# Delta-rule chunk outputs: adding the masked product onto the query's product in PSUM, with the sum copied by ScalarE

## Chip, cores and metric

One core of one Trainium2 chip. The metric is the device time of one execution in microseconds (us); given are the median of three runs of the kernel before and one profiled execution.

## What is computed

A hybrid block on x of 8 x 1024 x 128 floats: delta-rule attention, a mixture of 8 experts (top 2), a linear recurrence, and the experts again, each on a layer-normed x and added to it. The change touches the delta rule alone. Per batch row and head (4 heads, keys of 16, values of 32) the reference goes through the sequence in chunks with a state S:

```
def step(S, xs):
    qc, kc, vc, bc = xs
    kb = kc * bc[:, None]
    A = jnp.tril(kb @ kc.T, -1)
    U = solve_triangular(eye + A, vc * bc[:, None] - kb @ S, lower=True)
    o = qc @ S + jnp.tril(qc @ kc.T) @ U
    return (S + kc.T @ U, o)
```

Then o is normalised per head, multiplied by a gate, projected and added to x. The kernel cuts the sequence into chunks of 32, which gives the same outputs.

## The kernel before

Eight groups of 128 positions of all eight batch rows go through a software pipeline. An iteration i of it has 42 slots (SLOTS), and for each slot every engine runs, in a fixed order written out in its own loop, the pieces of several groups that are due in that slot: the state's chunks of group i (`stage_c`), the routing of group i-1 to the experts (`stage_r`, from iteration 1 on), what follows the state (`post`), the triangular inverse of group i+1 (`row_of_inverse` and `stage_b` on VectorE, `apply`), projections and grams of group i+2 (`stage_a`) and layer norm and convolution of group i+3 (`stage_l`). The tables from L_VAR to R_SEND (lines 339 to 382) say in which slot a piece stands. No scheduler moves anything: each engine works strictly through its own list, and semaphores do the rest.

A group has four chunks, which start in slots 2, 11, 24 and 29 (C_AT), in the last group in 2, 6, 10 and 14. One chunk goes like this:

- slot +0 (k = 0), TensorE L1675: 32 small matmuls of 32 x 32 weights give w S (columns WS0, 0 to 63) and q S (columns QS0, 64 to 127) in PSUM banks 0 to 3. It waits for the state (`d_S`) and for the copy of the chunk before (`d_oq`).
- slot +0, VectorE L868: vp = u - w S.
- slot +0, ScalarE L1354: when vp is done, copy q S from PSUM to `oq` (`d_oq`).
- slot +2, TensorE L1686 (KV): the state's product k^T vp into columns 0 to 63 of the same banks, after `d_vp` and `d_oq`; not for the last chunk of all. Then L1698 (PV): the masked product gp vp into bank 4 (BK_O), which it shares with the transposes of wk (L1658).
- slot +2, VectorE L874: S = masked KV + S, two instructions (`d_S`).
- slot +6 (in the last group +3), VectorE L880: o = oq + PV.

Later ScalarE squares o (L1369), VectorE reduces it, multiplies it with the gate (L895) and with the inverse norm (L899), TensorE turns and projects it (L1712, L1717), VectorE adds it to x (L905).

Beside this stand the pieces that the prediction follows. VectorE computes the inverse of group i+1 row by row: in slots 1 to 15 a product (L817) and a reduction (L821), with the state's pieces written between the two; in eight later slots the block products (L826 to L844). ScalarE in slot 14 writes the eight routing rows of group i-1 (L1271, `ysc`), in slot 16 rounds a piece of the experts' weights (L1405, `hl`; VectorE's L1063 follows), in slot 17 copies the turned rows (L1383, `yTf`); TensorE's router (L1739) follows, and VectorE takes its logits in slot 18 (L915, `lg`). In slot 27 ScalarE copies the turned queries of group i+2 (L1327, `qT`) and makes the masked `kqm` (L1329); TensorE's convolution (L1594) of group i+3 in slot 30 needs these to be out of PSUM bank 7, and it stands ahead of the fourth chunk's slot +2. In slots 34, 35, 36 and 40 TensorE makes the grams (L1630), which VectorE reads (L798, L800).

Of the kernel before, what the change touches and what calls it, by code (L numbers as in the profile page):

```python
# [80 lines left out]
def hybrid_kernel(nc, ap, out, phases=4):  # L81
# [37 lines left out]
    with ctx:  # L119
# [108 lines left out]
        S = sb1("S", [2, Q, 2 * DV])  # L228
        oq = sb1("oq", [2, 2, HEADS * DV])
        u = sb1("u", [2, BPB, HEADS * DV])  # L230
# [131 lines left out]
        C_S = 2  # L362
        C_PV = 2
        C_O = (6, 3)
        P_SQ = ((30, 1), (10, 18))
# [361 lines left out]
        def _(ve):  # L727
# [128 lines left out]
            def stage_c(g, t):  # L856
                for c in range(CG):
                    k = t - C_AT[last(g)][c]
                    at = g * CG + c
                    both = slice(2 * c, 2 * c + 2)  # L860

                    def by_pair(v):
                        return v.rearrange("p n (a d) -> p (n a) d", d=2 * DV)

                    if k == C_V:
                        ve.wait_ge(s("d_ws"), at + 1)
                        ve.wait_ge(s("d_uw"), at + 1)
                        ve.tensor_tensor(by_pair(vp[:, at % 2]), by_pair(u[:, g % 2, both]), ps[:, 0:4, WS0:WS0 + 2 * DV],  # L868
                                         ALU.subtract).then_inc(s("d_vp"), 1)
                    if k == C_S and at + 1 < NCK:  # L870
                        ve.wait_ge(s("d_kv"), at + 1)
                        for h in range(2):
                            cols = slice(DV * h, DV * h + DV)
                            ins = ve.scalar_tensor_tensor(S[:, (at + 1) % 2, :, cols], ps[:, 0:4, KV0 + DV * h:KV0 + DV * h + DV],  # L874
                                                          head_of[:, h, 0:1], S[:, at % 2, :, cols], ALU.mult, ALU.add)
                        ins.then_inc(s("d_S"), 1)
                    if k == C_O[last(g)]:
                        ve.wait_ge(s("d_pv"), at + 1)
                        ve.wait_ge(s("d_oq"), at + 1)
                        ve.tensor_tensor(o[:, g % 2, both], oq[:, at % 2],  # L880
                                         ps[:, BK_O, 0:2 * P].rearrange("p (n d) -> p n d", n=2), ALU.add)\
                            .then_inc(s("d_o"), 1)

            def post(g, half, t):
# [3 lines left out]
                if t == P_SS[last(g)][half]:  # L888
# [4 lines left out]
                        .then_inc(s("d_oss"), 1)  # L893
                if t == P_GATE[last(g)][half]:
                    marks["gs"] = ch.mark(ve.tensor_tensor(gs4, gs4, o4, ALU.mult))  # L895
                if t == P_O[last(g)][half]:
# [358 lines left out]
        def _(act):  # L1255
# [91 lines left out]
            def stage_c(g, t):  # L1347
                for c in range(CG):
                    if t == C_AT[last(g)][c] + C_V:
                        at = g * CG + c  # L1350
                        act.wait_ge(s("d_vp"), at + 1)
                        if at >= 2:
                            act.wait_ge(s("d_o"), at - 1)
                        act.copy(oq[:, at % 2].rearrange("p n (a d) -> p (n a) d", d=2 * DV), ps[:, 0:4, QS0:QS0 + 2 * DV])\  # L1354
                            .then_inc(s("d_oq"), 1)

# [216 lines left out]
        def _(pe):  # L1573
# [24 lines left out]
            def stage_a(g, t):  # L1598
# [23 lines left out]
                if t in A_GRAM:  # L1622
# [3 lines left out]
                    if g >= 2 and c == 0:  # L1626
                        pe.wait_ge(s("d_S"), (g - 1) * CG + 1)
                    for j in range(Q):
                        for a in range(4):
# [5 lines left out]
            def apply(g, late, t):  # L1635

                for k in range(2):
# [16 lines left out]
                    if t == WT[order][k]:  # L1654
                        pe.wait_ge(s("d_uw"), at + 1)
                        pe.wait_ge(s("d_wTs"), at)
                        pe.wait_ge(s("d_o"), g * CG + max(c - 1 - last(g), 0))
                        pe.transpose(ps[:, BK_O, 0:P], wk[:, c % 2].rearrange("p n d -> p (n d)"), ident[:, :])\  # L1658
# [6 lines left out]
            def chunk(g, c, k):  # L1665
                at = g * CG + c
                if k == 0:
                    pe.wait_ge(s("d_S"), at + 1)
                    pe.wait_ge(s("d_wTs"), at + 1)
                    pe.wait_ge(s("d_oq"), at)  # L1670
                    pe.wait_ge(s("d_gp"), min(g + 2, B) * CG)
# [6 lines left out]
                if k == C_KV:  # L1678
                    pe.wait_ge(s("d_vp"), at + 1)
                    pe.wait_ge(s("d_oq"), at + 1)  # L1680
                    if at + 1 < NCK:
# [7 lines left out]
                        ins.then_inc(s("d_kv"), 1)  # L1689
                if k == C_PV:  # L1690
                    pe.wait_ge(s("d_vp"), at + 1)
                    pe.wait_ge(s("d_o"), at)
                    pe.wait_ge(s("d_wTs"), g * CG + min(c + 2 + last(g), CG))
                    for n in range(2):
                        for h in range(HEADS):
                            k0 = n * P + h * DV
                            for j in range(Q):
                                ins = pe.matmul(ps[rows_of(j), BK_O, k0:k0 + DV], gp[rows_of(j), g % 3, 2 * c + n, h, :],  # L1698
                                                vp[rows_of(j), at % 2, n, h * DV:h * DV + DV], start=True, stop=True,
                                                skip_group_check=True)  # L1700
                    ins.then_inc(s("d_pv"), 1)

# [245 lines left out]
```

## Time and profile before

| | |
|---|---|
| median of 3 runs | 1392.16 us (1390.52 to 1394.14) |
| the profiled execution | 1395.43 us, its span 1393.5 us |
| mean granted TensorE clock | 0.802 of full |
| busy share of the span | TensorE 72%, VectorE 79%, ScalarE 51%, GpSimd 57% |
| last start of a chunk's vp | 556.2 us into the span |

The delta stage fills about the first 575 us. How to read the rows below: a timeline row has start, duration, engine, line, operation, output<-inputs, shape and count; in brackets the idle time of that engine just before it and who ended it. PE is TensorE, PEld its weight loads, DVE VectorE, ACT ScalarE, POOL GpSimd; L numbers are lines of the kernel before. TensorE's ends are modelled. Several like instructions in a row are merged into one row.

### The profile page before, as it was taken

To read this page: it belongs to the slowest core of one execution; us is meant where nothing else is said; L and a number is where in the kernel's file an instruction comes from. 1 tells how busy PE (TensorE), PEld (TensorE's weight loads), DVE (VectorE), ACT (ScalarE), POOL (GpSimd) and SP (SyncE) were. 2 spreads that over 40 slices of the span, in tenths; PEclk is the share of its full clock that TensorE was granted. 3 is DMA by queue.
4 is the path that set the end of the run, shared out by engine and by line. 5 is a ranking of instruction groups with operands and counts; after the bars stand their busy time and mean duration, and the time that the engine had idled before them with its cause. 6 is when DMAs were issued, how large, how long until landed. Compare 5 with 4: busy or idle time off the path is not lost.

```text
span 1393.5 us, 33043 instructions
## 1 busy us (share of the span) xinstructions
PE 997.9 (72%) x11963; PEld 732.8 (53%) x11963; DVE 1099.6 (79%) x3207; ACT 717.0 (51%) x1534; POOL 789.7 (57%) x670
## 2 busy tenths in 40 slices
PE   4547778677686546799999955656554699999960
PEld 1214455545555444678888842323232478788850
DVE  1188899989999894589788845898988689888845
ACT  2434253443534211467677735656565367677740
POOL 3331346556665544467777651158777747777650
PEclk9778778595876555699999986776676699999985
DMA  5010111111211104059778832122111659788839
GB/s 137 23 46 25 35 38 60 36 49 40 67 53 36 58 15 179 26 199 306 254 274 296 280 114 90 33 83 73 34 37 40 217 189 291 249 286 282 284 107 349
DMA packets 78625, 184.34 MB, mean 132 GB/s; under 512 B 16735, under 2 KB 44826, under 8 KB 68224
## 3 DMA queue, kind: packets, MB, share of 16 engines
q1 hardware_dynamic: 51280, 142.04, 30.5%
q0 software_dynamic: 17280, 35.70, 7.3%
q10 hardware_dynamic: 9904, 4.49, 1.2%
q8 instruction: 97, 1.59, 0.5%
q14 instruction: 64, 0.52, 0.1%
HBM read 131.20 MB, written 52.79 MB: 132 GB/s over the span
## 4 chain that ended last, share of the span: by engine, by line
PE 31%; DVE 28%; POOL 15%; issue 12%; ACT 7%; DMA 4%; SPq 1%; POOLq 0%; DVEq 0%; ACTq 0%
POOL xs L647 6%; PE ps L1594 5%; POOL res L690 5%; POOL rn L630 2%; PE ps L1810 2%; PE ps L1812 2%; PE ps L1811 2%; PE ps L1822 2%; PE ps L1824 2%; PE ps L1823 2%; DVE prod L817 2%; DVE t_p L821 2%; ACT ysc L1271 1%; DVE r_stats L739 1%; DVE hidl L1129 1%
## 5 line engine op out<-in xcount | busy, mean ns | idle before, releaser
L690 POOL DMA_INDIRECT res<-orow,idt x284 | 294.1, 1036 | 126.1 <-issue 80.6
L647 POOL DMA_INDIRECT xs<-ysc,slot_u x256 | 283.2, 1106 | 144.7 <-issue 72.8
L1129 DVE TENSOR_TENSOR hidl<-hidf,hidh 128x512 fp32r<-128x512 f32 (+1 forms) x320 | 199.1, 637 | 22.7 <-ACT hidh L1456 16.9
L1454 ACT ACTIVATE hidf<-ps,wb 128x512 f32<-128x512 f32 (+1 forms) x320 | 198.3, 655 | 5.0 <-PE ps L1812 4.4
L1810 PE MATMUL ps<-yTh,wb 128*128 128x512 f32 (+1 forms) x320 | 126.8, 396 | 0.0
L1822 PE MATMUL ps<-hidh,wb 128*128 128x512 f32 (+1 forms) x320 | 124.6, 389 | 0.0
L1812 PE MATMUL ps<-yTh,wb 128*128 128x512 f32 (+1 forms) x320 | 119.3, 373 | 0.0
L1811 PE MATMUL ps<-yTl,wb 128*128 128x512 f32 (+1 forms) x320 | 119.0, 372 | 0.0
L1824 PE MATMUL ps<-hidh,wb 128*128 128x512 f32 (+1 forms) x320 | 117.8, 368 | 0.0
L1823 PE MATMUL ps<-hidl,wb 128*128 128x512 f32 (+1 forms) x320 | 117.5, 367 | 0.0
L619 POOL TENSOR_TENSOR rstd<-rstd,neg_half 128x8 f32<-128x8 f32 x16 | 27.3, 1708 | 149.0 <-DVE rstd L746 149.0
L1464 ACT ACTIVATE out_t<-ps,wb 128x512 f32<-128x512 f32 (+1 forms) x80 | 51.4, 642 | 114.3 <-PE ps L1824 114.3
L630 POOL TENSOR_TENSOR rn<-ss,neg_half 128x64 f32<-128x64 f32 x8 | 85.9, 10742 | 31.8 <-DVE ss L770 31.8
L1456 ACT ACTIVATE hidh<-ps,wb 128x512 fp32r<-128x512 f32 (+1 forms) x160 | 103.1, 644 | 0.0
L637 POOL TENSOR_TENSOR ro<-ro,neg_half 128x16 f32<-128x16 f32 x16 | 50.8, 3177 | 59.8 <-DVE ro L892 59.6
L1874 PE MATMUL ps<-lin,w_rkv 128*128 128x512 f32 x96 | 63.7, 821 | 29.3 <-issue 27.9
L1271 ACT ACTIVATE y<-x,shift,rstd 128x128 f32<-128x128 f32 x128 | 51.0, 483 | 61.2 <-POOL shift L620 61.2
L1594 PE MATMUL ps<-yT,tap 128*128 128x512 f32 x128 | 73.8, 729 | 6.7 <-ACT kqm L1329 4.6
L1137 DVE TENSOR_TENSOR orow<-ps,wts 128x512 f32<-128x512 f32 (+1 forms) x80 | 50.0, 625 | 27.4 <-DMA res<-orow,idt 18.4
L1865 PE MATMUL ps<-ident,y 128*128 128x128 f32 x64 | 23.1, 438 | 62.1 <-ACT y L1271 56.4
L1128 DVE CAST hidh<-hidf 128x512 fp32r<-128x512 f32 (+1 forms) x160 | 67.5, 422 | 0.0
L1812 PEld LDWEIGHTS ps<-yTh,wb 128*128 128x128 f32 x320 | 61.1, 191 | 11.5
(265 smaller groups left out, 2565.6 us busy)
## 6 DMA issues: line engine op xcount, KB each, us to landing
wb<-wblob SPq DMA_DIRECT2D x80, 1032.0 KB, 6.2
xt<-xs SPq DMA_DIRECT2D x62, 288.0 KB
wblob<-hl SPq DMA_DIRECT2D x16, 512.0 KB
fin<-res SPq DMA_DIRECT2D x14, 512.0 KB, 10.5
hidf<-res SPq DMA_DIRECT2D x10, 512.0 KB, 4.1
res<-orow,idt POOLq DMA_INDIRECT x284
xs<-ysc,slot_u POOLq DMA_INDIRECT x256
rs<-res SPq DMA_DIRECT2D x8, 512.0 KB, 4.3
```

The source lines that it names most:

```text
L630: pool.tensor_tensor(rn[:, :, :], ss[:, :, :], neg_half[:, 0:2 * HEADS * BPB].rearrange("p (n h) -> p n h", n=BPB), ALU.pow).then_inc(s("d ...
L647: pool.indirect_dma_start(xs[:, :], bass.IndirectOffsetOnAxis(slot_u[:, g % 2, k, n:n + 1], 0), ysc[:, g % 2, n, :], None).then_inc(s(f"mo ...
L690: pool.indirect_dma_start(res[m][:, :], bass.IndirectOffsetOnAxis(idt[:, t % IR, j:j + 1], 0), orow[:, t % OR, j, :], None, bounds_check=2 ...
L1129: ve.tensor_tensor(hidl[:, t % 2, c, 0:n], hidf[:, t % 2, c, 0:n], hidh[:, t % 2, c, 0:n].bitcast(F32), ALU.subtract)\
L1454: ins = act.activation(hidf[:, t % 2, c, 0:n], ps[:, c, 0:n], ACT.Gelu_apprx_tanh, bias=b_col)
L1594: ins = pe.matmul(ps[:, BK_A, :].rearrange("p (j t) -> p j t", j=Q), tap[:, k, :], yT[:, g % 2, r, :, k:k + P], start=k == 0, stop=k == 3)
L1810: pe.matmul(ps[:, c, 0:n], high, yTh[:, t % 2, 0:n], start=True, stop=False)
L1811: pe.matmul(ps[:, c, 0:n], high, yTl[:, t % 2, 0:n], start=False, stop=False)
L1812: pe.matmul(ps[:, c, 0:n], low, yTh[:, t % 2, 0:n], start=False, stop=True).then_inc(sm("fc"), 1)
L1822: pe.matmul(ps[:, 5, 0:n], high, hidh[:, t % 2, c, 0:n], start=(c == 0), stop=False)
L1823: pe.matmul(ps[:, 5, 0:n], high, hidl[:, t % 2, c, 0:n], start=False, stop=False)
L1824: ins = pe.matmul(ps[:, 5, 0:n], low, hidh[:, t % 2, c, 0:n], start=False, stop=(c == HC - 1))
```

## The change

The masked product is written onto q S in PSUM instead of into bank 4, so that TensorE's accumulation makes the sum; ScalarE then copies the sum to `o`. `oq`, its copy and VectorE's addition go. In slot +2 TensorE runs PV first, waits until it is done (`d_pv`, its own semaphore), then runs KV. ScalarE's copy stands in slot +3 and waits for PV and for the state update that reads the same banks (`d_S`). TensorE's next chunk waits for that copy (`d_o`) where it waited for `oq`; the grams and the gate get a wait for `d_o`, the transposes of wk lose theirs.

```
-        C_PV = 2
-        C_O = (6, 3)
+        C_O = (3, 3)
...
-                    if k == C_O[last(g)]:
-                        ve.wait_ge(s("d_pv"), at + 1)
-                        ve.wait_ge(s("d_oq"), at + 1)
-                        ve.tensor_tensor(o[:, g % 2, both], oq[:, at % 2],
-                                         ps[:, BK_O, 0:2 * P].rearrange("p (n d) -> p n d", n=2), ALU.add)\
-                            .then_inc(s("d_o"), 1)
...
                 if t == P_GATE[last(g)][half]:
+                    ve.wait_ge(s("d_o"), g * CG + 2 * half + 2)
...
-                    if t == C_AT[last(g)][c] + C_V:
+                    if t == C_AT[last(g)][c] + C_O[last(g)]:
                         at = g * CG + c
-                        act.wait_ge(s("d_vp"), at + 1)
-                        if at >= 2:
-                            act.wait_ge(s("d_o"), at - 1)
-                        act.copy(oq[:, at % 2].rearrange("p n (a d) -> p (n a) d", d=2 * DV), ps[:, 0:4, QS0:QS0 + 2 * DV])\
-                            .then_inc(s("d_oq"), 1)
+                        act.wait_ge(s("d_pv"), at + 1)
+                        if at + 1 < NCK:
+                            act.wait_ge(s("d_S"), at + 2)
+                        act.copy(o[:, g % 2, 2 * c:2 * c + 2].rearrange("p n (a d) -> p (n a) d", d=2 * DV), ps[:, 0:4, QS0:QS0 + 2 * DV])\
+                            .then_inc(s("d_o"), 1)
...
                     if g >= 2 and c == 0:
                         pe.wait_ge(s("d_S"), (g - 1) * CG + 1)
+                        pe.wait_ge(s("d_o"), (g - 1) * CG)
...
-                        pe.wait_ge(s("d_o"), g * CG + max(c - 1 - last(g), 0))
                         pe.transpose(ps[:, BK_O, 0:P], wk[:, c % 2].rearrange("p n d -> p (n d)"), ident[:, :])\
...
-                    pe.wait_ge(s("d_oq"), at)
+                    pe.wait_ge(s("d_o"), at)
...
                 if k == C_KV:
                     pe.wait_ge(s("d_vp"), at + 1)
-                    pe.wait_ge(s("d_oq"), at + 1)
+                    for n in range(2):
+                        for h in range(HEADS):
+                            col0 = QS0 + DV * (h % 2)
+                            for j in range(Q):
+                                ins = pe.matmul(ps[rows_of(j), 2 * n + h // 2, col0:col0 + DV], gp[rows_of(j), g % 3, 2 * c + n, h, :],
+                                                vp[rows_of(j), at % 2, n, h * DV:h * DV + DV], start=False, stop=True,
+                                                skip_group_check=True)
+                    ins.then_inc(s("d_pv"), 1)
+                    pe.wait_ge(s("d_pv"), at + 1)
                     if at + 1 < NCK:
...
-                if k == C_PV:
-                    pe.wait_ge(s("d_vp"), at + 1)
-                    pe.wait_ge(s("d_o"), at)
-                    pe.wait_ge(s("d_wTs"), g * CG + min(c + 2 + last(g), CG))
```

How it stands on the engines (semaphores in brackets are what an instruction waits for; the changed kernel's lines are some 7 to 11 lower). On TensorE, third and fourth chunk of the first group with the convolution between them, before:

```order
L1675 MATMUL ps<-S,qT 32x64 x16
L1686 MATMUL ps<-vp,kn 32x64 [waits d_oq,d_vp]
L1686 MATMUL ps<-vp,kn 32x64 x15
L1698 MATMUL ps<-vp,gp 32x32 [waits d_wTs,d_o,d_vp]
L1698 MATMUL ps<-vp,gp 32x32 x31
L1619 MATMUL ps<-ident,qn 128x128 [waits d_kqTs,d_yT,d_kn]
L1619 MATMUL ps<-ident,qn 128x128 x3
L1675 MATMUL ps<-S,wT 32x64 [waits d_oq,d_gp,d_wTs,d_S]
L1675 MATMUL ps<-S,wT 32x64 x15
L1675 MATMUL ps<-S,qT 32x64 x16
L1594 MATMUL ps<-yT,tap 128x512 [waits d_kqTs,d_h,d_yT,taps]
```

and now:

```order
L1668 MATMUL ps<-S,qT 32x64 x16
L1677 MATMUL ps<-vp,gp 32x32 [waits d_vp]
L1677 MATMUL ps<-vp,gp 32x32 x31
L1687 MATMUL ps<-vp,kn 32x64 [waits d_pv]
L1687 MATMUL ps<-vp,kn 32x64 x15
L1612 MATMUL ps<-ident,qn 128x128 [waits d_kqTs,d_yT,d_kn]
L1612 MATMUL ps<-ident,qn 128x128 x3
L1668 MATMUL ps<-S,wT 32x64 [waits d_o,d_gp,d_wTs,d_S]
L1668 MATMUL ps<-S,wT 32x64 x15
L1668 MATMUL ps<-S,qT 32x64 x16
L1587 MATMUL ps<-yT,tap 128x512 [waits d_kqTs,d_h,d_yT,taps]
```

The masked product (vp,gp) has moved ahead of the state's product (vp,kn), which waits for it.

On ScalarE, slots 9 to 17 of iteration 1 (second chunk), before:

```order
L1271 ACTIVATE y<-x,shift,rstd 128x128 x7
L1354 COPY oq<-ps 128x256 [waits d_o,d_vp]
L1345 COPY wT<-ps 128x128 [waits d_wT]
L1271 ACTIVATE ysc<-x,r_shift,r_rstd 128x128 [waits moe_rstd]
L1271 ACTIVATE ysc<-x,r_shift,r_rstd 128x128 x7
L1405 CAST hl<-raw 128x512 [waits p_out,p_in]
L1383 COPY yTf<-ps 128x512 [waits moe_yT] x2
```

and now:

```order
L1264 ACTIVATE y<-x,shift,rstd 128x128 x7
L1338 COPY wT<-ps 128x128 [waits d_wT]
L1347 COPY o<-ps 128x256 [waits d_S,d_pv]
L1264 ACTIVATE ysc<-x,r_shift,r_rstd 128x128 [waits moe_rstd]
L1264 ACTIVATE ysc<-x,r_shift,r_rstd 128x128 x7
L1398 CAST hl<-raw 128x512 [waits p_out,p_in]
L1376 COPY yTf<-ps 128x512 [waits moe_yT] x2
```

The copy has moved behind wT and stands directly ahead of the routing rows; it waits for the state update.

On ScalarE, slots 23 to 33 of the same iteration (third and fourth chunk), before:

```order
L1329 ACTIVATE kqm<-ps,head_of 128x4x128 x2
L1354 COPY oq<-ps 128x256 [waits d_o,d_vp]
L1327 COPY qT<-ps 128x512 [waits d_o,d_gp,d_kqT]
L1329 ACTIVATE kqm<-ps,head_of 128x4x128 x2
L1354 COPY oq<-ps 128x256 [waits d_o,d_vp]
L1369 ACTIVATE osq<-o 128x512 [waits d_oss,d_o]
L1293 ACTIVATE hS<-ps 128x4x4x32 [waits d_proj,d_conv] x2
```

and now:

```order
L1322 ACTIVATE kqm<-ps,head_of 128x4x128 x2
L1347 COPY o<-ps 128x256 [waits d_S,d_pv]
L1320 COPY qT<-ps 128x512 [waits d_o,d_gp,d_kqT]
L1322 ACTIVATE kqm<-ps,head_of 128x4x128 x2
L1362 ACTIVATE osq<-o 128x512 [waits d_oss,d_o]
L1347 COPY o<-ps 128x256 [waits d_S,d_pv]
L1286 ACTIVATE hS<-ps 128x4x4x32 [waits d_proj,d_conv] x2
```

The third chunk's copy keeps its place in the list, but from slot 24 it is now in slot 27 and waits for the state update of slot 26; the fourth chunk's has moved behind osq.

## Rows read from the trace of the kernel before

**Rows 1.** Busy time by stretch: start:end, length, then busy (xinstructions) per engine, granted clock.

```profile
120.00:480.00 360.00, 260.90 (x6923) 181.29 (x6910) 330.21 (x989) 151.51 (x450) 205.66 (x118) 0.74 0.15 48
```

**Rows 2.** VectorE's waits from 120 to 560 us: total us, times, longest.

```profile
DVE n_c L798 <- PE ps L1630: 12.4, 17, 2.1
DVE S L874 <- PE ps L1686: 7.3, 7, 2.4
```

**Rows 3.** Timeline, VectorE, slot 8 of iteration 2: start, duration, then the instruction.

```profile
244.77 0.28 DVE L817 TENSOR_TENSOR prod<-t_p,n_p 128x128 f32<-128x128 f32 x1
...
244.97 0.41 DVE L880 TENSOR_TENSOR o<-oq,ps 128x256 f32<-128x256 f32 x1
...
245.30 0.28 DVE L821 TENSOR_REDUCE t_p<-prod 128x16 f32<-128x128 f32 x1
```

**Rows 4.** Timeline, first chunk of iteration 3, slots 2 to 4.

```profile
298.17 0.42 DVE L868 TENSOR_TENSOR vp<-u,ps 128x256 f32<-128x256 f32 x1
...
299.14 0.55 PE L1686 MATMUL ps<-vp,kn 32*32 32x64 f32 x32 [1.16 <-ACT oq L1354]
...
299.53 0.79 PE L1698 MATMUL ps<-vp,gp 32*32 32x32 f32 x64
...
299.80 0.61 DVE L874 SCALAR_TENSOR_TENSOR S<-ps,head_of,S 128x128 f32<-128x128 f32 x2
```

**Rows 5.** Timeline, iteration 2, slots 13 to 18: routing rows, state update, router, logits.

```profile
252.11 3.19 ACT L1271 ACTIVATE ysc<-x,r_shift,r_rstd 128x128 f32<-128x128 f32 x8 [0.22 <-POOL r_shift L620]
...
253.54 0.60 DVE L874 SCALAR_TENSOR_TENSOR S<-ps,head_of,S 128x128 f32<-128x128 f32 x2
...
258.13 3.58 PE L1739 MATMUL ps<-routerT,yTf 128*128 128x8 f32 x16 [0.68 <-ACT yTf L1383]
...
262.16 0.21 DVE L915 COPY lg<-ps 128x64 f32<-128x64 f32 x1
```

**Rows 6.** Timeline, iteration 2, slots 26 to 31; then the convolutions of iterations 3 and 4.

```profile
274.38 0.59 DVE L874 SCALAR_TENSOR_TENSOR S<-ps,head_of,S 128x128 f32<-128x128 f32 x2
274.44 0.58 ACT L1327 COPY qT<-ps 128x512 f32<-128x512 f32 x1 [2.97 <-PE ps L1619]
...
274.93 1.27 ACT L1329 ACTIVATE kqm<-ps,head_of 128x512 f32<-128x512 f32 x2
...
276.45 5.73 PE L1594 MATMUL ps<-yT,tap 128*128 128x512 f32 x8 [0.22 <-ACT kqm L1329]
...
282.38 0.83 PE L1698 MATMUL ps<-vp,gp 32*32 32x32 f32 x64
282.70 0.61 DVE L874 SCALAR_TENSOR_TENSOR S<-ps,head_of,S 128x128 f32<-128x128 f32 x2 [1.18 <-PE ps L1686]
...
336.82 6.28 PE L1594 MATMUL ps<-yT,tap 128*128 128x512 f32 x8
...
398.08 4.65 PE L1594 MATMUL ps<-yT,tap 128*128 128x512 f32 x8
```

**Rows 7.** Timeline, iteration 6, the same chain as in rows 5.

```profile
490.67 3.19 ACT L1271 ACTIVATE ysc<-x,r_shift,r_rstd 128x128 f32<-128x128 f32 x8 [0.90 <-POOL r_shift L620]
490.95 0.61 DVE L874 SCALAR_TENSOR_TENSOR S<-ps,head_of,S 128x128 f32<-128x128 f32 x2
...
499.79 0.23 DVE L915 COPY lg<-ps 128x64 f32<-128x64 f32 x1 [0.60 <-PE ps L1739]
```

**Rows 8.** Timeline, the last group's chunks two to four and the routing rows after them.

```profile
547.03 0.61 DVE L874 SCALAR_TENSOR_TENSOR S<-ps,head_of,S 128x128 f32<-128x128 f32 x2 [2.39 <-PE ps L1686]
...
554.14 0.60 DVE L874 SCALAR_TENSOR_TENSOR S<-ps,head_of,S 128x128 f32<-128x128 f32 x2
...
554.80 0.53 PE L1675 MATMUL ps<-S,wT 32*32 32x64 f32 x32 [1.35 <-DVE S L874]
...
558.90 1.08 PE L1698 MATMUL ps<-vp,gp 32*32 32x32 f32 x64
559.48 3.18 ACT L1271 ACTIVATE ysc<-x,r_shift,r_rstd 128x128 f32<-128x128 f32 x8
```

More of the change, by code:

```diff
@@ L228, in hybrid_kernel @@
         S = sb1("S", [2, Q, 2 * DV])
-        oq = sb1("oq", [2, 2, HEADS * DV])
         u = sb1("u", [2, BPB, HEADS * DV])
@@ L1689, in chunk @@
                         ins.then_inc(s("d_kv"), 1)
-                if k == C_PV:
-                    pe.wait_ge(s("d_vp"), at + 1)
-                    pe.wait_ge(s("d_o"), at)
-                    pe.wait_ge(s("d_wTs"), g * CG + min(c + 2 + last(g), CG))
[L1694 to L1701, printed above, removed]
             def post(g, half, t):
```

## Prediction

> **What bounds the kernel now.** The change sits in the delta stage, the first 575 us, so I read by stage: busy time in a window first, then who waits for whom, then the order of time around one chunk. In the window from 120 to 480 us VectorE is busy 330.21 of 360 us, ScalarE 151.51 [rows 1]. VectorE is the bound there, and what it waits for is small: the grams 12.4 us, the state's product 7.3 us [rows 2]. So an instruction taken off VectorE may be worth its duration, and a new wait of VectorE costs its whole length. The additions that go last 0.41 us each [rows 3]. The question is what each one stood beside, and how near its limit everything is that moves.
>
> **What goes: 32 additions on VectorE.** Four per group, in slots 8, 17, 30 and 35, and four in the last group. In slot 8 the addition stands between a product of the inverse and the reduction that needs it: the product starts at 244.77 and lasts 0.28, the addition starts at 244.97, the reduction at 245.30 [rows 3]. Without the addition the reduction waits for the product until 245.05, plus some 0.04 for the handover: 0.2 us saved, not 0.41. Seven groups: 1.4. The addition of slot 17 stands just as much between a reduction and its reader, and a wait right behind it (below) swallows the saving in all groups that route; slot 30's falls into a stretch that TensorE will set (below) in five groups; slot 35's falls ahead of the wait for the grams [rows 2]. The few left I put at 0.9. Sum: **-2.3 us**.
>
> **TensorE: 32 more matmuls ahead of the state's product.** Before, the state's product (L1686, KV) ran first and the masked product (L1698, PV) behind it, where nobody needed it for some slots. Now PV runs first, then TensorE waits for its own semaphore, then KV. What is queued behind is KV, and VectorE's state update S (L874) waits for it. In exchange KV's wait for the old ScalarE copy goes.
> First chunk of a group (slots 2 to 4) [rows 4]: vp ends at 298.59, PV can start 0.06 later (as from S's end at 554.74 to L1675 at 554.80 [rows 8]), so 298.65; its 64 pieces take 0.79 [rows 4] to 299.44; the own-semaphore handover no row shows. Nearest are 0.11 from KV's end at 299.69 to S [rows 4] and those 0.06 [rows 8]; waiting on oneself may cost more, so 0.06 to 0.4, an estimate, and I take 0.15, near the first. KV then starts at 299.59 instead of 299.14, and S, which now starts 0.11 after KV with no reserve, comes 0.45 later. The other first chunks look alike: 7 x 0.45 = **+3.2 us**.
> That adding into PSUM takes longer than writing into it no row of this product shows; I take the same 0.79, and as the upper end the 1.08 of a slower place [rows 8].
> In slots 13 and 26 S starts well after its product; there the delay is nearly covered by VectorE's own work.
>
> **ScalarE: the copy moves three slots and waits for S.** Before, it stood in the chunk's own slot and waited for vp; now it stands in slot +3 and waits for PV and S. What is queued behind it on ScalarE is what counts, and twice that is urgent.
> Slot 14: right behind it come the eight routing rows ysc [rows 5]. They started at 252.11, when GpSimd was ready; now the copy first waits for the second chunk's S, which ends at 254.14, then takes some 0.33 to the next start and 0.05 of handover, so ysc starts at 254.52, 2.41 later. Everything after it in this chain was back to back (ysc, hl, yTf, the router's L1739) and VectorE took the logits at 262.16, 0.45 after L1739's end at 261.71 [rows 5]. The logits now come at 261.71 + 2.41 plus a handover of 0.05 to 0.1, at 264.2: **2.0 us** of new wait, part of it already at hl in slot 16. Five groups (routing groups 0 to 4) have this shape. In the sixth VectorE already waited 0.60 for the logits; S ended there at 491.56, 0.89 after ysc's old start at 490.67 [rows 7], and with the copy's 0.38 and 0.4 that S comes later by PV, ysc is held 1.7. Sum 5 x 2.0 + 1.7 = **+11.7 us**.
> Slot 27: right behind the third chunk's copy come qT and the two kqm, and the convolution L1594 of slot 30 waits for these, ahead of the fourth chunk's PV and KV on TensorE. Before [rows 6]: S ends at 274.97, but qT had started at 274.44 and kqm ended at 276.20, the convolution started at 276.45. Now: 274.97 + 0.05 + 0.33 (copy) + 1.76 (qT to kqm's end) + 0.25 = 277.36, 0.91 later. Behind the convolution comes PV, 0.83, and the handover, 0.15, before KV. S of slot 31, for which VectorE already waited 1.18, comes 0.91 + 0.98 = 1.9 later. Five groups have a convolution there: **+9.5 us**.
>
> A rule speaks to this wait. KV, which writes other columns than the old copy read, waited for that copy all the same (1.16 us, "ACT oq" [rows 4]). The Trainium skill, in "PSUM — Partial Sum Buffer", section "PSUM bank collisions raise a hardware error", says that two engines must not be in one bank and quadrant at once, reads and different columns included. The trace agrees so far as that wait goes. By columns alone the copy would need only PV, and the sum would lose most of the 11.7 and the 0.91 x 5; with the rule, and with the wait that the diff writes out, it keeps them.
>
> **The last group** has no inverse work to hide in; its chunks follow each other (slots 2, 6, 10, 14) [rows 8]. Its second S (547.03, waited for 2.39) gets PV and handover ahead: +1.25. Twice the next chunk's L1675 now waits for the copy that follows S: 2 x 0.42. At the end ysc (559.48) stands behind the last copy, which waits for PV until 558.90 + 1.08 = 559.98 and takes 0.37: +0.9. Sum **+3.0 us**.
>
> **Sum**: -2.3 + 3.2 + 11.7 + 9.5 + 3.0 = +25.1 us. The profiled execution took 1395.43, so 1420.5 by its own time; it lies 3.27 above the median of the runs, 1392.16, hence **1417.3 us**, 1.8% slower.
> Ends: the convolution of slot 30 took from 4.65 to 6.28 us in the five groups [rows 6]; all five at the one or the other end, against a middle of 5.5, make -4.2 or +3.9. The handover at 0.06 or 0.4 in 13 places: -1.2 or +3.3. PV at 1.08 instead of some 0.8 in 12 places: +3.3. The last group at 1.25 alone: -1.75. All low ends together give 1410, all high ends 1428.
>
> **Rivals.**
> (a) *ScalarE's place costs nothing*: it has over 200 us free in 360 [rows 1], and if the chains behind slots 14 and 27 had more room than the rows show, only TensorE's order would be felt: 3.2 + 5 x 0.98 + 1.25 - 2.3 - 1.0 (slot 17) = +6.1, 1398. Against: the router's chain has 0.45 us of room [rows 5], and qT's has none [rows 6].
> (b) *Faster*: VectorE is the bound, and its relief counts in full. 32 x 0.41 = 13.1 us off: 1379. What decides is whether S can start no later than now; that needs a reserve of about 0.45 us behind KV. For it speaks the 330 of 360 us; against it that S starts 0.11 after KV's end in the first chunk [rows 4] and already waits in the fourth [rows 6]. By the Trainium skill's "TensorEngine Tiling (Array Packing)", section "PSUM Bottleneck", both ScalarE and VectorE should empty PSUM, which points this way; the trace shows VectorE loaded as that rule presumes, but also that the additions sit in gaps.
> (c) *Nothing*: the waits fall into waits of VectorE that I have not placed, and relief cancels the rest: 1392.
> (d) *The clock*: TensorE's granted clock averages 0.74 of full here [rows 1]; more idle time ahead of the convolution could leave all of slots 0 to 4 and 26 to 31 at 1.2 GHz. The high ends of convolution and PV (+7.2), and as much again in the other matmuls VectorE waits for: 1432.
>
> **How the numbers follow.** Forecast 0.72, (a) 0.13, (b) 0.07, (c) 0.04, (d) 0.04. A difference below 0.3%, about 4.2 us, can't be told from none. Slower are the forecast, (a) and (d): 0.89; same 0.04; faster 0.07. The range runs from just under (a) to the upper end of the forecast: 1397 to 1428.
>
> **What would show it.** In the profile after: VectorE's wait for S about 7.3 + 3 + 10 us, in the first and fourth chunks; a new wait of VectorE for ScalarE's hl and for the router's logits of some 2 us, six times; ysc released by S rather than by GpSimd; the convolution of slot 30 released by kqm each time; the delta stage's end some 25 us later and the experts' stages unchanged. Wrong would be a logits wait that stays near 0.6 us (then (a)), or a group period that shrinks by over 1 us (then (b)).

## The result and the profile after

The changed kernel takes **1417.17 us** (median of 4 runs, 1416.04 to 1419.97), the kernel before 1393.15 beside it (4 runs, 1390.52 to 1396.40): ratio 1.0169, 95% interval 1.0142 to 1.0197. The forecast was 1417.3 us, slower. The profiled execution of the changed kernel took 1416.04 us, its span is 1414.3, 20.8 above the span before. From the first vp to the routing rows that follow the last group the delta stage takes 458.79 us in place of 435.31 (+23.5); what comes after it takes 831.7 in place of 834.0, and lies between 829.6 and 834.0 in thirteen profiled executions of this study, so those -2.3 lie within its spread and are not shown to come from the change. Terms below are held against the +23.5.

Line numbers in the rows below are those of each run's own kernel. In the changed kernel vp is L866, S is L872, the masked product PV L1677, the state's product KV L1687, a chunk's first product L1668 and ScalarE's copy L1347.

First VectorE's waits in the changed kernel from 120 to 585 us (total us, times, longest), which answer to [rows 2], and the same window as [rows 1].

```profile
DVE S L872 <- PE ps L1687: 30.9, 16, 5.7
DVE n_c L796 <- PE ps L1624: 12.3, 17, 1.7
...
DVE lg L908 <- PE ps L1728: 6.3, 6, 2.0
DVE hl L1056 <- ACT hl L1398: 5.8, 5, 1.2
```

```profile
120.00:480.00 360.00, 251.74 (x6412) 167.45 (x6403) 306.63 (x929) 146.31 (x439) 192.92 (x106) 0.74 0.14 43
```

VectorE is busy 306.63 us of the window in place of 330.21, not because it was relieved by so much, but because the same work now takes longer than the window. Its wait for the state's product rose from 7.3 to 30.9 us, two waits are new (the logits, but for the 0.60 of [rows 7], and hl, which ScalarE casts behind the routing rows), the wait for the grams did not move. Where the time went by place, from vp's start of one chunk to the next, summed over the groups (from the timeline of both kernels):

| stretch | change, us | forecast for it |
|---|---|---|
| first chunk to second, seven groups | +3.5 | +3.2 of PV, less 1.4 of relief |
| second to third (slots 11 to 24) | +11.5 | +11.7, relief swallowed |
| third to fourth | +0.7 | 0 |
| fourth to the next group's first | +6.6 | +9.5, less some relief |
| last group, to its routing rows | +1.2 | +3.0 |

Now the three places. First chunk of iteration 3 in the changed kernel (start, duration, instruction), against [rows 4]:

```profile
307.99 0.42 DVE L866 TENSOR_TENSOR vp<-u,ps 128x256 f32<-128x256 f32 x1
...
308.46 0.98 PE L1677 MATMUL ps<-vp,gp 32*32 32x32 f32 x64 [0.65 <-DVE vp L866]
...
309.51 0.41 PE L1687 MATMUL ps<-vp,kn 32*32 32x64 f32 x32
310.09 0.61 DVE L872 SCALAR_TENSOR_TENSOR S<-ps,head_of,S 128x128 f32<-128x128 f32 x2 [0.49 <-PE ps L1687]
```

PV stands between vp and KV. It ends at 309.44, KV starts 0.07 later: that is TensorE's wait for its own semaphore. S, without a wait here before, waits 0.49; 0.35 to 0.91 in iterations 1 to 6.

Iteration 2, slots 13 to 18, against [rows 5]:

```profile
259.31 0.60 DVE L872 SCALAR_TENSOR_TENSOR S<-ps,head_of,S 128x128 f32<-128x128 f32 x2
260.00 0.37 ACT L1347 COPY o<-ps 128x256 f32<-128x256 f32 x1 [3.29 <-DVE S L872]
260.27 3.19 ACT L1264 ACTIVATE ysc<-x,r_shift,r_rstd 128x128 f32<-128x128 f32 x8
...
264.00 0.69 DVE L1056 TENSOR_TENSOR hl<-raw,hl 128x512 fp32r<-128x512 f32 x1 [1.15 <-ACT hl L1398]
...
269.91 0.22 DVE L908 COPY lg<-ps 128x64 f32<-128x64 f32 x1 [0.85 <-PE ps L1728]
```

ysc started 1.43 us ahead of S before, now 0.96 behind S's start, right after the copy that S releases. VectorE pays at hl (1.15) and at the logits (0.85): 2.0 together, five times.

Iteration 2, slots 26 to 31, against [rows 6]:

```profile
282.12 0.60 DVE L872 SCALAR_TENSOR_TENSOR S<-ps,head_of,S 128x128 f32<-128x128 f32 x2
282.81 0.37 ACT L1347 COPY o<-ps 128x256 f32<-128x256 f32 x1 [4.60 <-DVE S L872]
283.08 0.59 ACT L1320 COPY qT<-ps 128x512 f32<-128x512 f32 x1
...
283.44 0.53 PE L1668 MATMUL ps<-S,wT 32*32 32x64 f32 x32 [1.84 <-ACT o L1347]
283.56 1.28 ACT L1322 ACTIVATE kqm<-ps,head_of 128x512 f32<-128x512 f32 x2
...
283.74 1.00 PE L1668 MATMUL ps<-S,qT 32*32 32x64 f32 x32
...
285.10 5.95 PE L1587 MATMUL ps<-yT,tap 128*128 128x512 f32 x8 [0.35 <-ACT kqm L1322]
...
290.98 0.75 PE L1677 MATMUL ps<-vp,gp 32*32 32x32 f32 x64
...
291.79 0.41 PE L1687 MATMUL ps<-vp,kn 32*32 32x64 f32 x32
292.60 0.61 DVE L872 SCALAR_TENSOR_TENSOR S<-ps,head_of,S 128x128 f32<-128x128 f32 x2 [3.65 <-PE ps L1687]
```

From S's end to the convolution's start it is 2.37 us in all five groups; it was 1.27 to 1.58. From the convolution's end to the fourth chunk's S it is 1.33 to 1.56, and was 0.51. The two rows of L1668 matter later: the next chunk's first product waits for the copy too, and it ends at 284.74, just 0.36 ahead of the convolution.

### The profile page after: what moved, and what is told of

Read it like the earlier page. It is cut to its first block, busy times and chain, and to the rows that moved or that the text cites. A ratio compares the mean times of both kernels' runs of the same rounds, so it can differ in the third digit from the quotient of the medians.

```text
span 1414.3 us, 32923 instructions
## 1 busy us (share of the span) xinstructions
PE 998.9 (71%) x11963; PEld 726.3 (51%) x11963; DVE 1090.3 (77%) x3175; ACT 716.8 (51%) x1534; POOL 791.7 (56%) x670
## 4 chain that ended last, share of the span: by engine, by line
PE 32%; DVE 24%; POOL 15%; issue 12%; ACT 9%; DMA 5%; SPq 1%; POOLq 0%; ACTq 0%; DVEq 0%
POOL xs L645 6%; POOL res L688 5%; PE ps L1587 5%; ACT ysc L1264 2%; POOL rn L628 2%; PE ps L1728 2%; PE ps L1799 2%; PE ps L1801 2%; PE ps L1800 2%; PE ps L1811 2%; PE ps L1813 2%; PE ps L1812 2%; DMA res<-orow,idt 2%; DVE r_stats L737 1%; PE ps L1677 1%
## 5 line engine op out<-in xcount | busy, mean ns | idle before, releaser
L628 POOL TENSOR_TENSOR rn<-ss,neg_half 128x64 f32<-128x64 f32 x8 | 86.0, 10744 | 30.9 <-DVE ss L768 30.9
L1347 ACT COPY o<-ps 128x256 f32<-128x256 f32 x32 | 12.0, 376 | 123.1 <-DVE S L872 122.7
L1720 PE MATMUL ps<-ident,ysc 128*128 128x128 f32 x128 | 32.4, 381 | 50.0 <-ACT yTf L1376 34.6
```

Of the source, the lines that this page charges most:

```text
L628: pool.tensor_tensor(rn[:, :, :], ss[:, :, :], neg_half[:, 0:2 * HEADS * BPB].rearrange("p (n h) -> p n h", n=BPB), ALU.pow).then_inc(s("d ...
```

## The experiments

Each ratio is to the kernel before, run on the same chip in the same rounds. "Delta stage" is the stretch named above in the profiled execution (435.3 before, 458.8 changed).

**1. The second chunk's copy behind the routing rows.** In the changed kernel:

```
-        C_O = (3, 3)
+        C_O = ((5, 19, 27, 32), (5, 9, 13, 17))
-                    if t == C_AT[last(g)][c] + C_O[last(g)]:
+                    if t == C_O[last(g)][c]:
```

> Edit: in the changed kernel ScalarE's copy of the second chunk moves from slot 14 to slot 19, behind the routing rows, the cast hl and yTf; nothing else. The theory (ScalarE's place): the copy holds ysc until S is done, and the chain behind it brings the logits late. Then VectorE's waits for hl and for the logits go (about 5.8 and 6.3 us in the changed kernel, 0.6 of it old), some 11.5 us less: 1405 to 1406. Rival (TensorE's order): the 64 pieces ahead of the state's product are what costs, the logits only show where it ends; then the wait comes back at the next late thing, VectorE's state update or the grams, and the time stays at 1414 to 1418.

Measured: 1404.35 us, ratio 1.0057 (1.0042 to 1.0072), so 0.0112 less than the change, some 16 us with an uncertainty of about 4; delta stage 448.8, 10.0 less (its profiled execution, 1406.55 us, lies 2.2 above its median). Iteration 2, slots 13 to 18:

```profile
259.43 3.19 ACT L1264 ACTIVATE ysc<-x,r_shift,r_rstd 128x128 f32<-128x128 f32 x8 [1.17 <-POOL r_shift L618]
260.86 0.60 DVE L872 SCALAR_TENSOR_TENSOR S<-ps,head_of,S 128x128 f32<-128x128 f32 x2
...
269.28 0.22 DVE L908 COPY lg<-ps 128x64 f32<-128x64 f32 x1
```

ysc is released by GpSimd again, and neither hl nor the logits keep VectorE waiting. From the second chunk's vp to the third's it is 19.53 to 19.55 us in iterations 1 to 4 where it was 21.72 to 21.73, and over the six iterations the stretch gets 12.6 shorter: the forecast's 11.7 of wait and the fifth of a microsecond of each addition that the wait had swallowed. The theory holds; its rival and rival (a) of the prediction fall. Between the fourth chunk and the next group 4.8 us are lost again; see experiment 9.

**2. The queries turned one slot earlier.** In the changed kernel:

```
-        A_KQT = (22, 26)
+        A_KQT = (22, 25)
```

> Edit: in the changed kernel the queries are turned one slot earlier (slot 25 on TensorE, 26 on ScalarE), so that qT and kqm stand ahead of the third chunk's copy; nothing else. The prediction's step as written: the convolution starts 0.91 us earlier in five groups, 1412.6. Another reading of the same step: the copy also holds the next chunk's first product (L1668), which waits for it and stands ahead of the convolution on TensorE; it ended at 284.74 in iteration 2, 0.35 us before the convolution's start at 285.10. Then 5 x 0.35 = 1.7 is all that comes back: 1415.4, and the convolution follows L1668 without a wait. Rival (the convolution's own time or TensorE's other work sets the fourth chunk): no change, 1417.

Measured: 1414.66 us, ratio 1.0144 (1.0124 to 1.0163), 0.0025 less than the change, which the two intervals can't tell from nothing, so the time does not decide between the two readings and the rival; delta stage 457.9, 0.9 less. The trace says more. Iteration 2:

```profile
283.13 0.60 DVE L872 SCALAR_TENSOR_TENSOR S<-ps,head_of,S 128x128 f32<-128x128 f32 x2
283.82 0.37 ACT L1347 COPY o<-ps 128x256 f32<-128x256 f32 x1 [2.05 <-DVE S L872]
...
284.45 0.53 PE L1668 MATMUL ps<-S,wT 32*32 32x64 f32 x32 [3.22 <-ACT o L1347]
...
285.64 4.83 PE L1587 MATMUL ps<-yT,tap 128*128 128x512 f32 x8
```

kqm is long done and the convolution now stands right behind L1668, which stands behind the copy. From S's end to the convolution it is 1.73 to 1.96 us, 0.4 to 0.6 less than in the change, not 0.9: the copy reaches the convolution over two paths, and the forecast saw one.

**3. A short masked product.** In the changed kernel; seven eighths of the masked product are left out.

```
-                    for n in range(2):
-                        for h in range(HEADS):
+                    for n in range(1):
+                        for h in range(1):
```

> Edit: in the changed kernel the masked product takes 4 small matmuls in place of 32, so seven eighths of the masked product are left out of the result; orders and waits stay. The theory: the product lasts some 0.1 us in place of 0.75 to 1.08, the state's product comes 0.7 earlier, VectorE's waits for S fall in the first chunks (0.35 to 0.91 now) to nothing and in the fourth (2.6 to 3.9 now) by 0.7, the last group by 1.25 to 2: 3.5 + 3.5 + 1.6 = 8.6 less, 1408 to 1409. Rival (ScalarE's place carries nearly all): 1414 or more, with the waits for S in the first chunks gone all the same but found again elsewhere.

Measured: 1403.95 us, ratio 1.0072 (1.0053 to 1.0090); delta stage 447.4, 11.4 less. The first chunk of iteration 3:

```profile
304.68 0.26 PE L1677 MATMUL ps<-vp,gp 32*32 32x32 f32 x8
...
305.03 0.41 PE L1687 MATMUL ps<-vp,kn 32*32 32x64 f32 x32
305.73 0.60 DVE L872 SCALAR_TENSOR_TENSOR S<-ps,head_of,S 128x128 f32<-128x128 f32 x2
```

In iterations 1 to 6 S waits no more in the first chunk. The gain is larger than the 8.6 expected, and the rival (1414 or more) falls: the first chunks give 3.8, the stretches from the fourth chunk to the next group 2.3, the last group 4.3 (27.2 to 22.9 us), the rest 1.0. In the last group TensorE's pauses are shorter too (in the second chunk's KV 0.93 us, 2.20 in the change), so how much of the 4.3 is PV's length is not shown.

**4. Only the relief.** In the kernel before, VectorE's addition is left out, ScalarE copies the query's product straight to o (the masked product is computed, and missing from the output), and the waits go by that copy's semaphore and, for PV's bank, by PV's own:

```
-                    if k == C_O[last(g)]:
-                        ve.wait_ge(s("d_pv"), at + 1)
-                        ve.wait_ge(s("d_oq"), at + 1)
-                        ve.tensor_tensor(o[:, g % 2, both], oq[:, at % 2],
-                                         ps[:, BK_O, 0:2 * P].rearrange("p (n d) -> p n d", n=2), ALU.add)\
-                            .then_inc(s("d_o"), 1)
...
-                        if at >= 2:
-                            act.wait_ge(s("d_o"), at - 1)
-                        act.copy(oq[:, at % 2].rearrange("p n (a d) -> p (n a) d", d=2 * DV), ps[:, 0:4, QS0:QS0 + 2 * DV])\
-                            .then_inc(s("d_oq"), 1)
+                        act.copy(o[:, g % 2, 2 * c:2 * c + 2].rearrange("p n (a d) -> p (n a) d", d=2 * DV), ps[:, 0:4, QS0:QS0 + 2 * DV])\
+                            .then_inc(s("d_o"), 1)
```

> Edit: in the kernel before, VectorE's addition is left out and ScalarE copies the query's product to the output as it stands, so the masked product is missing from the result although TensorE still computes it; orders stay. It measures the relief alone. The theory: the additions stand in gaps of dependent chains and beside other waits, 2.3 us less than the kernel before: about 1390.5. Rival (VectorE is the bound and its relief counts in full): 32 x 0.41 = 13.1 us less, 1379 to 1380.

Measured: 1390.58 us, ratio 0.9968 (0.9956 to 0.9980): 4.4 us, between 2.8 and 6.1; delta stage 434.3, 1.0 less. In slot 8 of iteration 2, against [rows 3]:

```profile
246.33 0.28 DVE L816 TENSOR_TENSOR prod<-t_p,n_p 128x128 f32<-128x128 f32 x1
...
246.65 0.29 DVE L820 TENSOR_REDUCE t_p<-prod 128x16 f32<-128x128 f32 x1
```

From the product's start to the reduction's it is 0.32 where it was 0.53. An addition of 0.41 that stood in a gap gives back 0.21; slots 11 to 24 get shorter by 0.21 too (19.75 to 19.54). Rival (b)'s 13.1 us are excluded.

**5. TensorE's order alone.** In the kernel before, the block of PV moves ahead of that of KV, nothing else:

```
+                if k == C_PV:
+                    pe.wait_ge(s("d_vp"), at + 1)
...
                 if k == C_KV:
                     pe.wait_ge(s("d_vp"), at + 1)
...
-                if k == C_PV:
-                    pe.wait_ge(s("d_vp"), at + 1)
...
```

> Edit: in the kernel before, the masked product is issued ahead of the state's product instead of behind it; it still goes to its own bank, VectorE still adds it, ScalarE's copies stay. It is TensorE's order alone, without accumulation, without the own-semaphore wait and without the move of the copies. The theory: first chunks 0.36 later each (0.06 + 0.79 of product in place of the 0.55 that the state's product waited anyway): 2.5; fourth chunks 5 x 0.8 = 4.0; last group 1.1: 7.6 us over the kernel before, ratio 1.0055. Rival: TensorE's order costs 13 us by itself, as the shortened masked product gave back: ratio 1.009 to 1.010. If the accumulation is what costs, the ratio stays at 1.002 or less.

Measured: 1397.30 us, ratio 1.0027 (1.0011 to 1.0042): 3.8 us, half of the expected 7.6, and the rival's 13 is excluded; delta stage 440.4, +5.1. S waits 15.9 us longer (23.2 in place of 7.3); part of it is given back where VectorE waits for the grams (12.4 to 10.8 us) and where its additions wait for PV (8.9 to 2.3 us). First chunk of iteration 4; in this kernel PV is L1686 and KV L1698:

```profile
359.94 0.42 DVE L868 TENSOR_TENSOR vp<-u,ps 128x256 f32<-128x256 f32 x1
360.41 0.75 PE L1686 MATMUL ps<-vp,gp 32*32 32x32 f32 x64 [0.60 <-DVE vp L868]
361.02 0.47 PE L1698 MATMUL ps<-vp,kn 32*32 32x64 f32 x32
...
361.59 0.61 DVE L874 SCALAR_TENSOR_TENSOR S<-ps,head_of,S 128x128 f32<-128x128 f32 x2
```

With no wait between them, and with the products in different banks, KV starts 0.61 after PV, ahead of PV's end; the changed kernel needs 0.81 for the same step at the same PV (290.98 to 291.79). So the own-semaphore wait costs 0.2 here; by PV's end, which is modelled, that is 0.06 of handover and 0.14 of lost overlap. Where the granted clock is 0.50 and PV takes 1.08, the step is 1.16 to 1.17 in place of 0.80 (third chunks), so the wait costs 0.37. Adding into PSUM costs nothing that can be seen: at a granted clock of 1.00 the undisturbed PV takes 0.75 in both. Taking the wait away was not tried, since both products write the same banks.

**6 to 8. The convolution elsewhere.** VectorE's dearest wait in the change is at the fourth chunk, behind the convolution. Experiment 6 moves `L_CONV` from (30, 34) to (32, 34) on top of experiment 1; experiment 7 to (35, 37), with `L_H` at (36, 37); experiment 8 makes the move to (32, 34) in the kernel before. In experiments 6 and 8, and in 7:

```
-        L_CONV = (30, 34)
+        L_CONV = (32, 34)
```

```
-        L_CONV = (30, 34)
+        L_CONV = (35, 37)
...
-        L_H = (33, 34)
+        L_H = (36, 37)
```

> Edit: the changed kernel with the second chunk's copy in slot 19 as in the first experiment, and in addition the first convolution moves from slot 30 to 32, behind the fourth chunk's masked and state's products. Theory: VectorE's waits for S in the fourth chunks (2.9 to 3.8 us each, five of them) go: 16 us less than the first experiment's 1404, 1388 to 1390. Rival: the convolution then stands right ahead of the grams on TensorE and the grams come as late as now; the wait moves from S to the grams' n_c, 1400 to 1404.

> Edit: as the experiment before, with the convolutions in slots 35 and 37 (and their readers on ScalarE in 36 and 37), behind the first of the grams. Theory: neither S nor the first n_c waits for a convolution: 1386 to 1390, below the kernel before. Rival: what reads the convolution (hS and the next projection, ahead of the first chunk's products) is late in its place, and VectorE waits in the first chunks or at the grams: 1396 to 1404.

> Edit: in the kernel before, the first convolution moves from slot 30 to 32, behind the fourth chunk's products; nothing else. The fourth chunks' waits for S are 3.4 us in sum there. Theory: they go, ratio 0.9975. Rival: they turn up at the grams: ratio 1.000, or above where the convolution is slower there.

Measured: 1404.99 us, ratio 1.0078 (1.0058 to 1.0099); 1442.10, 1.0348 (1.0324 to 1.0371); 1403.65, 1.0070 (1.0046 to 1.0093). All three theories fell, and experiment 7 came out far above its rival (1396 to 1404) too. VectorE's waits in experiment 6 from 120 to 585 us; in experiment 1 the same lines have 16.6 us at the grams and 28.9 at S:

```profile
DVE n_c L796 <- PE ps L1624: 28.3, 16, 4.8
DVE S L872 <- PE ps L1687: 11.8, 10, 5.3
```

The wait of 17 us at S goes, 12 of it stand at the grams, which queue behind the convolution on TensorE. In experiment 8 the waits at S shrink by 3 us and those at the grams grow from 12.4 to 26.4 [rows 2]. In experiment 7 the waits at S fall to 4.7 us, and the output projection (x) and hl come late instead:

```profile
DVE x L898 <- PE ps L1706: 35.8, 9, 5.7
DVE hl L1056 <- ACT hl L1398: 26.5, 6, 4.4
```

**9. Both moves of the copies' neighbours**: the edits of experiments 1 and 2 together.

> Edit: the changed kernel with both moves, the second chunk's copy in slot 19 and the queries turned one slot earlier. Theory: the two places of ScalarE's copy are apart from each other, so their gains add (1.0169 less 0.0112 and 0.0025): ratio 1.003 to 1.004, 1397 to 1399; what is left is TensorE's order, its wait for itself and the third chunk's copy ahead of L1668. Rival: the gains overlap, since TensorE sets the end of each group and takes one of them back at the grams: ratio 1.0055 or more.

Measured: 1404.44 us, ratio 1.0080 (1.0052 to 1.0108), no better than experiment 1 alone; delta stage 446.5, 2.3 below that of experiment 1, whose profiled execution lay 2.2 above its median. The gains don't add to the 1.003 to 1.004 expected; the rival, 1.0055 or more, fits. The grams of iteration 2 show something that takes from the gain in both experiments (TensorE's and VectorE's rows of the second gram):

```profile
299.36 0.41 PE L1624 MATMUL ps<-kqm,kT 32*32 32x128 f32 x6
301.48 0.49 PE L1624 MATMUL ps<-kqm,kT 32*32 32x128 f32 x26 [1.71 <-issue]
...
302.12 0.42 DVE L796 TENSOR_TENSOR n_c<-ps,nbeta 128x256 f32<-128x256 f32 x1 [2.31 <-PE ps L1624]
```

Amid 32 like matmuls TensorE stands still for 1.71 us and waits for nothing that the profile shows ("issue"). Then its granted clock falls, here by stretches (start:end, length, busy time of PE, PEld, DVE, ACT, POOL, then granted clock, DMA share, GB/s):

```profile
296.00:299.40 3.40, 3.19 (x123) 2.54 (x125) 2.39 (x6) 0.85 (x3) 2.53 (x3) 1.00 0.16 55
299.40:301.50 2.10, 0.39 (x9) 0.12 (x9) 0.41 (x1) 0.54 (x2) 1.75 (x2) 1.00 0.51 195
301.50:305.30 3.80, 3.80 (x95) 1.95 (x95) 3.15 (x4) 2.02 (x8) 0.41 (x1) 0.63 0.58 165
```

Ahead of the pause the clock is at its upper level (2.4 GHz), behind it the mean is 0.63, so for most of the stretch at the lower (1.2 GHz). In iterations 1 to 4 the stretch from the fourth chunk to the next group is 1.8 to 3.5 us longer with such a pause at the grams than without. It occurs in two groups each of experiments 1 and 9; in the changed kernel the longest there is 0.63 us, in the kernel before one of 1.46 stands in the first group. That the pauses fall elsewhere when the chain ahead is faster fits this and is not shown. What they are is open.

**10 and 11. A half convolution ahead.** On top of experiment 9 the first two taps of the first convolution go to slot 28, ahead of L1668, where TensorE stood idle. Experiment 11 makes this split and the earlier turning in the kernel before:

```
+        L_CONV0 = 28
-                for r in range(2):
-                    if t == L_CONV[r]:
+                for r, ks, at in ((0, (0, 1), L_CONV0), (0, (2, 3), L_CONV[0]), (1, (0, 1, 2, 3), L_CONV[1])):
+                    if t == at:
...
-                        for k in range(4):
+                        for k in ks:
...
-                        ins.then_inc(s("d_conv"), 1)
+                        if ks[-1] == 3:
+                            ins.then_inc(s("d_conv"), 1)
```

> Edit: the kernel of e9_both_moved, and the first half (two of four taps, four of eight matmul records) of the first convolution goes to slot 28, ahead of L1668, where TensorE stood idle from 280.44 to 283.41 in the changed kernel (but for the turning of the queries); the second half stays in slot 30. Theory: the fourth chunk's S comes up to 2.5 us earlier in five groups, its waits (1.9 to 3.3 us) nearly vanish: 8 to 11 us less than the kernel of e9, 1387 to 1391, below the kernel before. Rival: L1668 and vp come later by as much and TensorE is the bound of this stretch: no change against e9, or slower.

> Edit: the kernel before with the queries turned one slot earlier and the same split of the first convolution, without the change. It tells whether a gain in e10 belongs to the change. Theory: there is little to win, since the fourth chunk's S waits 3.4 us in all: ratio 0.997 to 0.999. Rival: L1675 is delayed and vp waits: ratio 1.002 or more.

Measured: 1397.72 us, ratio 1.0020 (0.9995 to 1.0045), for 10; **1390.52 us, ratio 0.9972** (0.9956 to 0.9987), for 11. The split does for the change most of what was hoped (0.0060 less than experiment 9, some 8 us) and doesn't bring it below the kernel before, where its theory had put it (1387 to 1391); without the change it is faster than both kernels, as its theory said. How much of that is the split and how much the earlier turning of the queries was not run apart. In experiment 11, iteration 2:

```profile
273.03 3.75 PE L1595 MATMUL ps<-yT,tap 128*128 128x512 f32 x4 [0.31 <-ACT kqm L1330]
...
276.72 0.52 PE L1677 MATMUL ps<-S,wT 32*32 32x64 f32 x32
...
277.75 2.28 PE L1595 MATMUL ps<-yT,tap 128*128 128x512 f32 x4
...
280.78 0.60 DVE L875 SCALAR_TENSOR_TENSOR S<-ps,head_of,S 128x128 f32<-128x128 f32 x2
```

The half of the convolution runs at a granted clock of 0.50 (3.75 us for four records, 2.28 at 0.86 for the other four) in what was idle time of TensorE, and S of the fourth chunk no longer waits (1.18 in [rows 6]).

## Why the prediction was right

The sign, the places and the sum were right, the sum (25.1 against 23.5 in the stage) partly because errors of some 1 to 3 us cancelled. That the median met the forecast to 0.1 us is luck.

**Relief, -2.3.** Right in kind: in slot 8 0.21 us instead of 0.41 (experiment 4). In time the relief alone measures 4.4 (2.8 to 6.1), so -2.3 was somewhat small; the profiled stage shows 1.0.

**First chunks, +3.2.** Too small, and in another term than feared. The handover was taken at 0.15 and is 0.06 to 0.07 there. PV, taken at 0.79, took 0.83 to 1.37 us in iterations 1 to 6, a mean of 1.07, which the sum's upper end (1.08) allowed for; in experiment 5 four of the six took 0.75 to 0.78. Accumulation is not the reason: in experiment 10, which accumulates likewise, the first five took 0.75. Nor is the clock, but in iteration 6 (0.50); in iterations 1 to 5 it was 1.00. In iteration 2 TensorE pauses for 0.42 within PV; what lengthens the others is open. KV starts 1.18 after vp on average where it started 0.56: 0.62 later a chunk instead of 0.45, and 1.22 in iteration 0; 6 x 0.62 + 1.22 = 4.9. The stretch grew by 3.5, with the relief in it.

**Slot 14, +11.7.** Right step by step. ysc starts 0.36 after S's end, with the copy of 0.37 between (forecast: 0.05 and 0.33); hl and the logits wait 1.15 + 0.85 = 2.0 five times; the sixth logits wait rose from 0.60 to 2.05. Moving the copy away gave 12.6 back in that stretch (experiment 1). This is the larger half of the loss.

**Slot 27, +9.5.** The size of the steps was right: the convolution starts 0.93 later (2.37 after S against a mean of 1.44; forecast 0.91), and the fourth chunk's S follows it 0.95 later (forecast 0.98). The convolutions themselves took 5.12 to 6.17, 0.6 more on average than before, which only the sum's end allowed for (+3.9). Together S comes 12.3 us later in these five groups, but the stretch to the next group grew by 8.8: behind S 3.4 come back, 2.4 of them in the first group, whose grams lost the pause of 1.46 us. So that 8.8 lies near 9.5 is in part luck. What failed is the path: "right behind the third chunk's copy come qT and the two kqm, and the convolution L1594 of slot 30 waits for these". It waits for them by only 0.34 to 0.57; L1668 waits for the copy as well, stands ahead of the convolution on TensorE, and holds it when qT is early (experiment 2). So the cure that this reading suggests moves the convolution by 0.4 to 0.6 of the 0.93. In iterations 5 and 6, for which nothing was forecast, that stretch changed by +0.05 and -2.25.

**Last group, +3.0.** It came to +1.2. Its S and L1668 wait in the places forecast (5.70 us for the second S, 1.47 and 1.84 for two copies), but pauses of TensorE rule there. In the changed kernel one stands in the second chunk's KV:

```profile
566.71 0.30 PE L1687 MATMUL ps<-vp,kn 32*32 32x64 f32 x4
569.21 0.39 PE L1687 MATMUL ps<-vp,kn 32*32 32x64 f32 x28 [2.20 <-issue]
...
569.75 0.61 DVE L872 SCALAR_TENSOR_TENSOR S<-ps,head_of,S 128x128 f32<-128x128 f32 x2 [5.70 <-PE ps L1687]
```

Before, the pause was 5.1 us long and fell into the first chunk's PV, where VectorE's addition waited 5.3 us for it:

```profile
540.56 0.33 PE L1698 MATMUL ps<-vp,gp 32*32 32x32 f32 x7 [5.12 <-issue]
...
540.95 0.42 DVE L880 TENSOR_TENSOR o<-oq,ps 128x256 f32<-128x256 f32 x1 [5.34 <-PE ps L1698]
```

The three waits of the additions for PV in this group, 8.9 us in all, went with the additions. The change and experiments 1, 2, 9 and 10 have the same order in this group and took 25.1 to 27.5 us in it, so +1.2 and +3.0 lie no farther apart than pauses alone move it.

**The rule on banks.** The copy reads the query's columns, S the state's, and the copy starts some 0.09 after S's end each time, because the diff writes that wait. That is where the loss at slot 14 comes from, as experiment 1 shows for what stands behind the copy, and 0.93 of the 2.46 us by which the fourth chunk's S is later in each of five groups; the rest of these is the convolution's length and PV with its handover. By the Trainium skill, "PSUM — Partial Sum Buffer", section "PSUM bank collisions raise a hardware error", two engines must not be in one bank and quadrant at once, reads included. That rules the shorter wait out; no run here tests it, since nothing was run with the two in one bank at once. KV's wait of 1.16 us in [rows 4] is written in the kernel before just as well, so it shows what that program does and is no test either.

**The rivals.** (a) is excluded by experiment 1, (b) by experiment 4. (c) is excluded by the interval. (d) is not needed as a whole: the granted clock from 120 to 480 us is 0.74 in both kernels. A part of its kind is there: over the five convolutions of slot 30 the clock was 0.59 to 0.71 where it had been 0.58 to 0.79, and they took 2.9 us longer in all.

## What to carry to other kernels

An operation that stands in the gap of a dependent chain is worth the gap's rest when it is removed, here half of its duration; measure that with a kernel that only leaves it out. When work moves to an engine with time to spare, look not at its busy share but at the instructions queued behind it there and at what releases it: a copy of 0.37 us that had to wait for VectorE cost 2 us in each of five groups. A wait that is moved off one queue often stands again at the next reader (experiments 6 to 8); what gained here was work put into TensorE's idle time ahead of the wait (experiments 10 and 11).

## What was not expected of the hardware

TensorE's wait for its own semaphore costs 0.06 to 0.09 us of idle time (0.30 in three chunks) and, with it, the overlap of two products into different banks: from PV's start to KV's 0.2 us at a granted clock of 1.00, 0.37 at 0.50. The 64 pieces of PV took 0.75 us at 1.00 and 1.08 at 0.50, the 32 of KV 0.41 and 0.53, so half the clock did not double them.

TensorE pauses for up to 2.1 us amid runs of like matmuls without any wait that the profile shows, and longer in the last group (5.1 us before, 2.2 in the change). The pauses fall in different places in kernels that differ in a few orders only, and can shift a kernel's time by a few microseconds. During the two long ones the DMA engines were busy nearly throughout (shares 0.94 and 1.02, 392 and 411 GB/s), during the gram pauses of experiments 1 and 9 the share was 0.22 to 0.57, but during one of 1.27 us in the last group's third PV of the change it was 0.00. So heavy transfers go with many of them and not with all, and nothing in this study shows what causes them.
